# A graph layer and a ternary feed-forward layer on one core: first and second stage divided anew

## What is computed

```python
# graph layer, on the layer-normalised x
msg_sum = segment_sum(x[src], dst)                 # sum over the edges that end in a node
deg     = segment_sum(ones, dst)                   # number of such edges
neigh   = msg_sum / maximum(deg, 1.0)[:, None]
h = x @ W_self + neigh @ W_neigh + b
h = where(h >= 0, h, 0.01 * h)
x = x_in + h / maximum(norm(h), 1e-12)
# feed-forward layer, on the layer-normalised x; weights quantised to -s, 0, s in groups of 128 inputs
s  = mean(abs(w_group)) + 1e-5;  wq = clip(round(w_group / s), -1, 1) * s
x = x + (silu(xn @ wq_gate.T) * (xn @ wq_up.T)) @ wq_down.T
```

## Time and profile before

| | us |
|---|---|
| median of 3 runs (386.08 to 388.95) | 386.58 |
| the profiled execution, its own time | 388.67 |
| its span | 386.8 |
| of it PE busy / DVE busy / ACT busy / POOL busy | 348.7 / 321.6 / 250.5 / 166.4 |
| first chunk product to the last, PE | 21.25 to 134.1 |
| `neighbour_sum` on DVE, n = 0, 1 and 9 | 151.43, 155.53 and 197.06 |
| granted TensorE clock, mean | 0.972 |

### The profile page before, as it was taken

How to read it: one execution, slowest core, us unless ns; L and a number is a source line. 1 busy time by engine, 2 the same in 40 slices (tenths; PEclk the granted TensorE clock), 3 DMA queues, 4 the chain that set the end, 5 groups by cost and what they waited for, 6 DMA issues and landing times.

```text
span 386.8 us, 5916 instructions
## 1 busy us (share of the span) xinstructions
PE 348.7 (90%) x1741; PEld 261.9 (68%) x1741; DVE 321.6 (83%) x748; ACT 250.5 (65%) x667; POOL 166.4 (43%) x214
## 2 busy tenths in 40 slices
PE   1989988979999899999975899999999999999972
PEld 1435544535554448777765789899899899889962
DVE  2598887977989502899968799999999999999983
ACT  2265757666777311577465787897897897788740
POOL 3011342221232110212001228588888879878982
PEclk9998999989999989999999999999999999999995
DMA  7941212222122100120000000000000000000034
GB/s 236 261 138 56 56 54 81 68 58 65 59 75 73 33 3 3 28 75 20 3 1 0 2 0 2 1 3 0 2 1 3 1 0 2 1 3 0 2 108 159
DMA packets 9415, 16.73 MB, mean 43 GB/s; under 512 B 1062, under 2 KB 1886, under 8 KB 9378
## 3 DMA queue, kind: packets, MB, share of 16 engines
q1 hardware_dynamic: 9378, 16.29, 14.9%
HBM read 13.73 MB, written 2.56 MB: 42 GB/s over the span
## 4 chain that ended last, share of the span: by engine, by line
PE 53%; DVE 24%; ACT 9%; POOL 5%; issue 5%; DMA 2%; POOLq 0%; SPq 0%; ACTq 0%; DVEq 0%
PE bank L1170 35%; PE bank L1061 6%; PE bank L1107 5%; DVE hot_dst L881 5%; DVE tq_gu L817 4%; ACT mag_early L628 3%; DVE hot_src L877 2%; POOL acc L599 2%; ACT hot_src L613 2%; DVE tq_d L817 2%; PE bank L1023 2%; PE bank L1091 2%; DMA w_sb<-in_L_gnn_W_neigh 2%; DVE bn L922 1%; DVE x_sb L919 1%
## 5 line engine op out<-in xcount | busy, mean ns | idle before, releaser
L1170 PE MATMUL bank<-x_hi,t_gu 128*128 128x378 f32 (+1 forms) x264 | 95.8, 363 | 2.0 <-DVE x_lo L936 1.3
L1170 PE MATMUL bank<-x_lo,t_gu 128*128 128x378 f32 (+1 forms) x264 | 94.6, 358 | 0.0
L1061 PE MATMUL bank<-w_sb,xnT 128*125 128x512 f32 x160 | 88.4, 640 | 1.4 <-DMA w_sb<-in_L_gnn_W_neigh 1.4
L599 POOL TENSOR_TENSOR acc<-acc,d_one 128x378 f32<-128x378 f32 (+1 forms) x84 | 88.3, 1077 | 0.7 <-ACT d_one L728 0.3
L561 POOL TENSOR_SCALAR thr<-absum 128x4 f32<-128x4 f32 (+1 forms) x34 | 12.2, 358 | 129.5 <-ACT mag_early L628 89.5
L1023 PEld LDWEIGHTS bank<-hot_dst,hot_src 128*125 128x125 bf16 x281 | 32.0, 139 | 52.0 <-DVE hot_dst L881 33.5
L971 DVE SCALAR_TENSOR_TENSOR g_acc<-bank,nscale,g_acc 128x378 f32<-128x378 f32 (+1 forms) x99 | 63.9, 646 | 3.7 <-PE bank L1170 3.3
L586 POOL TENSOR_TENSOR hh<-sg,u_acc 128x378 f32<-128x378 f32 (+1 forms) x32 | 35.2, 1100 | 66.4 <-ACT sg L750 62.6
L971 DVE SCALAR_TENSOR_TENSOR u_acc<-bank,nscale,u_acc 128x378 f32<-128x378 f32 (+1 forms) x99 | 63.6, 642 | 0.0
L1170 PEld LDWEIGHTS bank<-x_hi,t_gu 128*128 128x128 f32 x264 | 50.2, 190 | 6.7 <-DVE x_lo L936 2.0
L1170 PEld LDWEIGHTS bank<-x_lo,t_gu 128*128 128x128 f32 x264 | 50.4, 191 | 3.6
(11 more groups left out here) (107 smaller groups left out, 548.3 us busy)
## 6 DMA issues: line engine op xcount, KB each, us to landing
raw<-in_L_ffn_w_gate SPq DMA_DIRECT2D x11, 256.0 KB, 2.9
raw<-in_L_ffn_w_up SPq DMA_DIRECT2D x11, 256.0 KB, 2.6
out_x<-x_sb SPq DMA_DIRECT2D x10, 224.0 KB
raw<-in_L_ffn_w_down SPq DMA_DIRECT2D x8, 256.0 KB, 2.6
x_sb<-in_x SPq DMA_DIRECT2D x1, 1344.0 KB
w_sb<-in_L_gnn_W_neigh SPq DMA_DIRECT2D x1, 1024.0 KB, 7.1
w_sb<-in_L_gnn_W_self SPq DMA_DIRECT2D x1, 1024.0 KB, 8.6
raw<-in_L_ffn_w_down SPq DMA_DIRECT2D x4, 192.0 KB, 2.3
```

The lines of the kernel that those rows point to most:

```text
L599: nc.gpsimd.tensor_tensor(to, to, d_one[:, o, slot, 0:width(u)], ALU.add).then_inc(d_added, 1)
L1061: last = nc.tensor.matmul(to[0:TP, :], xnT[:, t, k * TP:(k + 1) * TP], w_sb[:, k, half * D:(half + 1) * D], start=k == 0, stop=k == KD - 1)
L1170: last = nc.tensor.matmul(to, w, parts[h], start=h == 0, stop=h == 1)
```

## The change

1. **Degree sums inside the first stage.** The rows are cut by node tiles (`DEG`: tiles 0 to 2, 3 to 5, 6 to 9). The first two are summed after slots 36 and 57 and turned into columns after slots 39 and 60, all in bank 7. The third follows in the second stage, between n = 0 and n = 2. DVE inverts tiles 0 to 5 ahead of n = 0 and tiles 6 to 9 in n = 2.
2. **The flag** is read by DVE as soon as it is made, and by PE at slot 8. The conditional jump stays where it was.
3. **Loads.** 14 of 34 loads (56 jobs) stay in the first stage, and 20 (76 jobs) go to the second, 3 for each n up to n = 6: DVE takes one after `neighbour_sum`, one after `residual` and one at the end of n; ACT makes one at the start of n and two behind `normalize1`.
4. **Own products.** Those of tile 9 move behind n = 0 of the second stage. Bank 6 alone now takes the own products.
5. **Bias.** POOL adds it to tile 0 behind load 13 and to tiles 1 to 9 in the second stage, behind the second threshold of each n. `nscale` is worked out once, for all 132 jobs, at the end.
6. `y_hi` is made at slot 6 of its own tile (before: slot 1 of the next); `neighbour_sum` reads banks 4 and 5, the transposed x1 goes through banks 0 and 1, and the ring of the third stage begins 2, 6, 1, 0, 4, 3, 5.

```diff
-    ROW = [(0, 418), (418, 416), (834, 416)]
-    ROW_BANK = [2, 3, 1]
+    DEG = [(0, 3), (3, 6), (6, NT)]
+    DEG_SLOT = [36, 57]
+    DEG_COL = 500
...
-        LOADS1 = 2 * NF + 3
+        Z1, Z2 = list(range(NT - 1)), [NT - 1]
+        z_place = {t: i for i, t in enumerate(Z1 + Z2)}
+        LOADS1 = 14
         JOBS1 = load_end[LOADS1 - 1]
...
-        def down_jobs(n):
-
-            lo, hi = (LOADS1 + max(0, min(NL, 3 * i // 2)) for i in (n, n + 1))
-            return range(load_end[lo - 1], load_end[hi - 1])
+        def late_jobs(i):
+
+            l = LOADS1 + i
+            return range(load_end[l - 1], load_end[l]) if LOADS1 <= l < len(loads) else range(0)
...
-        RING = [2, 6, 0, 1, 5, 3, 4]
+        RING = [2, 6, 1, 0, 4, 3, 5]
...
+        def degree_row(c):
+
+            a, b = DEG[c]
+            n = (b - a) * TP + (b - a) % 2
+            for s in range(NT):
+                last = nc.tensor.matmul(bank[7][0:2, 0:n], ones_r[0:TP, :], a_t[:, s, a * TP:a * TP + n],
+                                        start=s == 0, stop=s == NT - 1)
+            return last
...
+            def add_bias(t):
+
+                pool.wait_ge(z_out, z_place[t] + 1)
+                nc.gpsimd.tensor_tensor(z[:, t, :], z[:, t, :], bias_b[0:TP, :], ALU.add).then_inc(z_done, 1)
+
+            for l in range(LOADS1):
                 scales_of(l)
+            pool.wait_ge(bias_in, 16)
+            add_bias(0)
+            for n in range(NT):
+                for l in range(LOADS1 + 3 * n, min(LOADS1 + 3 * n + 3, len(loads))):
+                    if l == LOADS1 + 3 * n + 2:
+                        add_bias(n + 1)
+                    scales_of(l)
+                if LOADS1 + 3 * n + 2 >= len(loads) and n + 1 < NT:
+                    add_bias(n + 1)
+            nc.gpsimd.tensor_scalar(nscale[:, 0:JOBS], absum[:, 0:JOBS], 1.0 / P, Q_EPS, ALU.mult, ALU.add).then_inc(nscales, 1)
...
             for n in range(NT):
+                for j in late_jobs(3 * n):
+                    abs_of(j)
...
                     if n >= 2:
                         normalize1(n - 2)
-                for j in down_jobs(n):
+                for j in late_jobs(3 * n + 1):
                     abs_of(j)
+                if n < len(Z2):
+                    z_from_bank(Z2[n])
+                if n == 0:
+                    degree_out(2)
+                for j in late_jobs(3 * n + 2):
+                    abs_of(j)
+            act.wait_ge(nscales, 1)
...
+            link(nc.vector.tensor_scalar(flag[:], bank[5][:, 2 * NCP:2 * NCP + 1], float(E), None, ALU.is_lt))
+            any_outside = dve.value_load(flag[0:1, 0:1])
...
             for n in range(NT):
                 neighbour_sum(n)
+                for j in late_jobs(3 * n - 1):
+                    ternary_of(j)
                 if n >= 1:
                     residual(n - 1, between=n)
                 else:
                     leak(n)
+                for j in late_jobs(3 * n):
+                    ternary_of(j)
                 if n >= 2:
                     shift1(n - 2)
                 if n >= 4:
                     x1_low(n - 4)
-                for j in down_jobs(n - 1):
+                for j in late_jobs(3 * n + 1):
                     ternary_of(j)
+                if n == 2:
+                    inverse_degrees(DEG[2][0], DEG[2][1], 3, 2)
...
+                if slot in DEG_SLOT:
+                    c = DEG_SLOT.index(slot)
+                    pe.wait_ge(block_out, -(-DEG[c][1] * TP // WIN))
+                    degree_row(c).then_inc(deg_rows, 1)
+                if slot - 3 in DEG_SLOT:
+                    c = DEG_SLOT.index(slot - 3)
+                    pe.wait_ge(deg_row_out, c + 1)
+                    degree_columns(c).then_inc(deg_ready, 1)
...
             for n in range(NT):
+                pe.wait_ge(block_out, min(NB, -(-(n + 1) * TP // WIN)))
                 if n >= 2:
                     pe.wait_ge(hsum, n - 1)
...
+                if n < len(Z2):
+                    t = Z2[n]
+                    pe.wait_ge(z_out, z_place[t])
+                    for k in range(KD):
+                        own_product(t, k)
+                if n == 0:
+                    pe.wait_ge(block_out, NB)
+                    pe.wait_ge(rdeg_done, 1)
+                    degree_row(2).then_inc(deg_rows, 1)
+                if n == 1:
+                    pe.wait_ge(deg_row_out, 3)
+                    degree_columns(2).then_inc(deg_ready, 1)
```

More of the change, by code:

```diff
@@ L145, in gnn_ffn @@
     flag = small("flag", [P, 1], I32)
-    good = small("good", [P, 1], F32)
     bias_b = small("bias_b", [P, D], F32)
@@ new lines, in general_dve, with degree_columns @@
+                dve.wait_ge(gen_sum, 3)
+        def degree_row(c):
+            a, b = DEG[c]
+            n = (b - a) * TP + (b - a) % 2
+            for s in range(NT):
+                last = nc.tensor.matmul(bank[7][0:2, 0:n], ones_r[0:TP, :], a_t[:, s, a * TP:a * TP + n],
+                                        start=s == 0, stop=s == NT - 1)
+            return last
+        def degree_columns(c):
+            a, b = DEG[c]
+            for t in range(a, b):
+                last = nc.tensor.matmul(bank[7][0:TP, DEG_COL + t:DEG_COL + t + 1], deg_row[0:1, (t - a) * TP:(t - a + 1) * TP],
+                                        ones[0:1, 0:1], start=True, stop=True, skip_group_check=True)
+            return last
@@ new lines, in general_pe @@
+                with pe.Fori(0, GK) as k:
+                    pe.wait_ge(gen_out, 1 + k)
+                    for j in range(GC):
+                        pe.wait_ge(gen_hot, k * (GQ * GC) + j + 1)
+                        nc.tensor.matmul(bank[7][0:TP, 0:NT * GB], src_gen[:, 0:TP], hot_gen[:, 0:NT * GB],
+                                         start=j == 0, stop=False, skip_group_check=True).then_inc(gen_used, 1)
+                    with pe.Fori(1, GQ) as q:
+                        for j in range(GC):
+                            pe.wait_ge(gen_hot, (k * GQ + q) * GC + j + 1)
+                            nc.tensor.matmul(bank[7][0:TP, 0:NT * GB], src_gen[:, 0:TP], hot_gen[:, 0:NT * GB],
+                                             start=False, stop=False, skip_group_check=True).then_inc(gen_used, 1)
@@ L498, in gnn_ffn @@
+                pe.wait_ge(gen_out, 1 + GK)
+                for c in range(2):
+                    degree_row(c).then_inc(gen_sum, 1)
+                    pe.wait_ge(gen_taken, c + 1)
+                    last = degree_columns(c)
+                last.then_inc(gen_sum, 1)
         block = ctx.enter_context(nc.Block())
@@ L666, in _ @@
                             ACT.Copy).then_inc(block_out, 1)
-            for c, (s0, n) in enumerate(ROW):
-                act.wait_ge(deg_rows, c + 1)
-                nc.scalar.activation(deg_row[:, s0:s0 + n], bank[ROW_BANK[c]][0:2, 0:n], ACT.Copy).then_inc(deg_row_out, 1)
+                    if slot - 1 in DEG_SLOT:
+                        degree_out(DEG_SLOT.index(slot - 1))
             def root_of(t):
@@ L1015, in transpose_xn, with own_product @@
                 last.then_inc(done, 1)
+            def own_product(t, k):
+                last = nc.tensor.matmul(bank[6][0:TP, :], xnT[:, t, k * TP:(k + 1) * TP], w_s[:, k, :],
+                                        start=k == 0, stop=k == KD - 1)
+                if k == KD - 1:
+                    last.then_inc(z_ready, 1)
             def add_chunk(c):
```

242 lines of the change are left out of this document (91 added, 151 removed).

## The result

The changed kernel took 401.79 us (median of 4 runs, 399.34 to 402.47), the kernel before 386.44 (median of 4, 386.08 to 388.95). The ratio is 1.037, with a 95% interval of 1.033 to 1.042: slower, by some 15 us. The profiled execution took 401.65 us, its span is 399.8, the mean granted clock 0.96 (before: 388.67, 386.8, 0.972).

The account below looks back on a forecast made before the run. Took the first stage's waits between PE, ACT and DVE, then DVE's pace in the second stage, as the bound; 13.1 + 1.6 + 0.5 = +15.2 us on 388.7 is 403.9, less 2.1 for the median 401.8; range 388 to 409.

Parts of the forecast that it names:

- step a: First stage: 43 jobs leave, DVE's queue falls below PE's, and all 12.8 us of PE's waiting go.
- loosen the ties: First stage: jobs at 0.9 a slot, y_hi four slots before DVE wants it, nine bias additions gone; no separate size.
- The degree rows inside: First stage: two degree rows and their columns add twice 2.46 us, +4.9 us, on PE.
- step d: Between the stages: 2.1 us for flag read and jump stay on the path, all of it early; ends 0 and 4.2.
- Rival D: Between the stages: the jump keeps its 2.1 us and the early read costs as much: 403.9 us, chance 0.05.
- To n = 1: From the first stage's end at 125.0, PE's sums, own products and third degree row take 15.5 us, to 140.5.
- Second stage: n = 1 to 7: DVE waits for late loads and additions; steps sum to 59.0 us, n = 7 13.1 us late.
- the late threshold: Second stage: the last load's threshold follows normalize1 of the same n; DVE waits 1.5 to 2 us for ACT and POOL.
- Rival B: Second stage: last load in time, no addition in the way, DVE's own work sets 39.8 us: 381.0 us, chance 0.14.
- Rival A: Second stage: bias additions do not hold DVE, 8.9 us less: 392.9 us, chance 0.10.
- The clock's term: Ahead of the sums of n = 9: PE's wait lowers its clock, +1.6 us (0 to 3).
- the ring: Third stage: the fourth product waits for x1_low(6) instead of the seventh, +0.5 us (0 to 1.4).

Follow-up runs that it names:

- Part 5: y_hi early alone in the kernel before: 0.978; late again in the changed kernel with later jobs, additions in the first stage and 25 loads: 0.998 instead of 0.973.
- part 4: Changed kernel with later jobs and additions in the first stage, 20 or 25 instead of 14 loads there: 0.982 and 0.973, against 0.993 with 14.
- part 2: Kernel before with the flag read early on DVE and PE, the jump unchanged: ratio 0.997.
- the second run of part 1: Changed kernel with bias additions of tiles 0 to 8 back in the first stage, tile 9 behind the last threshold: 392.95 us, ratio 1.016.
- the third: Changed kernel with ternary jobs of late loads one place later on DVE and bias additions back in the first stage: 384.7 us, ratio 0.993.
- the later order: DVE takes each late load one place later; in the changed kernel, alone: 398.1 us, ratio 1.029.

## Why the prediction was right, and where it was not

**The forecast** of 401.8 us met 401.79, more closely than its steps deserve; the direction and the mechanism of the second stage were right, the last digit is luck. In profiled executions the difference is 401.65 - 388.67 = 13.0 us, and the sum had 15.2. The 2.1 us that it took off for the median made up for it: the profiled execution before lay 2.2 us above its median, the one after 0.1 below. The 15.2 and the 13.0 part like this: n = 1 came 3.45 us early, the steps to n = 7 were 0.4 longer, n = 7 to 9 0.2 shorter, and the third stage 1.1 longer.

**First stage: about the right size, the cause largely another.** 121.55 us against 125.0. The gain of waiting (step a) was said to come as 43 jobs leave and take DVE's queue below PE's. Part 5 shows `y_hi`'s place, with no load moved, to be worth 10.8 us at the end of the stage, and part 4 the eleven loads 1.9 once `y_hi` is early. What the leaving jobs would have given with `y_hi` late no run shows, since none has 14 loads and the old place. The prediction named the early `y_hi` in half a sentence among three things that "loosen the ties"; it took the bias additions for the one that matters, and with these back in the first stage n = 1 came no later (136.85 against 137.05). The row that would have told it is DVE's wait for `y_hi`, 7.3 us in 22 to 97, which I passed over because the 31.9 and 30.2 of the earlier trace rows are larger. Yet most of those stayed when it went (part 5), and the stage was 10.8 us shorter all the same.

**The small terms of that stage.** The degree rows inside took 1.94 and 1.97 us of busy time, the columns 0.81 each time, 5.5 us in all where the forecast has 4.9. The flag's read (step d) was counted with 2.1 us as staying on the path, and all of it went; that is most of the 3.45 us by which the stage ended early, and the other 1.3 was not followed up. Rival D, the jump, is refuted by part 2.

**To n = 1.** 15.5 us from the end of the stage, and 15.5 measured (121.55 to 137.05). Two of its terms missed and made up for each other: the own products of tile 9 took 3.0 us (126.54 to 129.57) instead of 3.4, the third degree row 2.7 (to 132.23) instead of 2.3.

**Second stage: right, and shown.** The steps of n = 1 to 6 are 8.3, 10.5, 9.8, 9.8, 9.5 and 11.6 us, 59.4 in all, where the forecast has 8.2, 10.4, 9.6, 9.6, 9.35 and 11.85, 59.0. Both mechanisms were tested apart: the addition's hold by the second run of part 1 (8.4 us, priced 8.9), and the late threshold by the third (another 8.7 with the addition out of the way). Rival B, 381.0, is what happens if both are gone: 384.7 measured. Its steps came out at 41.9 us instead of 39.8, and n = 7 to 9 took 14.1 us instead of 10.65, in part since the later order gives n = 7 a load; what the 2.1 us are was not followed up. Rival A's two terms, six times 1.05 and 2.5, add to 8.8 and not to 8.9.

**Behind it.** n = 7 to 9 took 12.0 us (forecast 10.65 + 1.6). The clock's term is in the trace: PE waited 4.61 us, and behind that, from 201.30 to 204.40, the granted clock was 0.52. The third stage is 1.6 us longer, where the forecast had 0.5 for the ring. By PE's third transposes of x1 in the stage 1.5 of it is there: from the stage's first product they are 21.15 us away (209.65 to 230.80), before 19.66 (198.23 to 217.89). PE's waits between the two sum to 6.8 us in both kernels, so no waiting was added in sum, the ring's included. What differs is products at the lower clock, which take 0.52 us instead of 0.34: the changed kernel has two stretches of them, of some 3 us each, and before has one. One product of each stretch of the changed kernel:

```profile
216.36 0.52 PE L1207 MATMUL bank<-x_hi,t_gu 128*128 128x378 f32 x1
...
226.34 0.52 PE L1207 MATMUL bank<-x_lo,t_gu 128*128 128x378 f32 x1
```

I had priced the clock ahead of n = 9 alone. This is read from one execution of each kernel, and no run tests it.

**What the prediction didn't ask.** It priced the order in which jobs were moved, and its rival B took for granted that moving them pays once nothing holds DVE; it never set the division of loads apart from `y_hi`. Part 4 answers for the orders tried here: with `y_hi` early it doesn't pay. A late load costs 0.7 us net even in the better order.

## What to carry to other kernels

Before moving work out of a stage, look for short waits of the engine that all others wait for: DVE's 7.3 us for `y_hi` stood below 60 us of larger waits, and one early copy gave 8.4 us where a redivision of the stages, with that copy in it, lost 15. The size of a wait doesn't say what it is worth. When work goes from one queue to another stage, walk through every queue it passes, here ACT, POOL and DVE for one load, and put a consumer one place behind the last producer; two holds in series show their full worth only when both are gone, so try them together as well as apart. And put POOL's element-wise work where DVE has slack or reads a bank, not in a row beside DVE's two-input work.
